# Order of work at three places of a fused macaron block: first block, and both borders between its stages

## What is computed

```python
def reference(x, Wk, bk, Wv, bv, ln_g, ln_b, Wo, bo, W_r, W_k, W_v, mu_r, mu_k):
    def ffn(x):                                   # x is layer-normalized
        x_prev = shift x by one token, zero first
        xr = mu_r * x + (1 - mu_r) * x_prev
        xk = mu_k * x + (1 - mu_k) * x_prev
        return sigmoid(xr @ W_r.T) * (square(relu(xk @ W_k.T)) @ W_v.T)
    def attn(x):                                  # quaternion memory
        keys = unit quaternions of x @ Wk.T + bk
        values = quaternions of x @ Wv.T + bv
        memory = cumsum(quat_mul(values, keys), axis=1)
        retrieved = quat_mul(memory, conj(keys)) / sqrt(position)
        normed = layernorm(retrieved) * ln_g + ln_b
        return x + (normed @ Wo.T + bo)
    x = x + 0.5 * ffn(layernorm(x))
    x = x + attn(layernorm(x))
    return x + 0.5 * ffn(layernorm(x))
```

## Time and profile before

| | us |
|---|---|
| runs of the kernel before: lowest, median, highest of 3 | 669.58, 671.86, 672.56 |
| the profiled execution | 670.52 |
| its span on the core | 668.8 |
| PE busy in the span | 619.1 (93%) |
| DVE, ACT, POOL busy | 561.3, 429.2, 545.2 |

### The profile page before, as it was taken

How to read it: one execution, slowest core, us unless ns; L and a number is a source line. 1 busy time by engine, 2 the same in 40 slices (tenths; PEclk the granted TensorE clock), 3 DMA queues, 4 the chain that set the end, 5 groups by cost and what they waited for, 6 DMA issues and landing times.

```text
span 668.8 us, 12336 instructions
## 1 busy us (share of the span) xinstructions
PE 619.1 (93%) x3412; PEld 524.6 (78%) x3412; DVE 561.3 (84%) x1170; ACT 429.2 (64%) x792; POOL 545.2 (82%) x626
## 2 busy tenths in 40 slices
PE   2899999999978999999999999999767999999997
PEld 2788988988856777777777777777546988998996
DVE  5889999997669999999999999999847877877773
ACT  4576776776456766666676666666354776776762
POOL 3498888887538999999999999999916788889864
PEclk9999999999998999999999999999877999999999
DMA  8730000000000000000000000000000101101111
GB/s 247 236 116 1 0 0 0 0 0 1 1 0 1 0 2 0 0 0 0 0 0 0 0 0 0 0 0 1 0 1 0 65 32 63 63 31 63 63 63 65
DMA packets 19257, 18.66 MB, mean 28 GB/s; under 512 B 1312, under 2 KB 19232, under 8 KB 19232
## 3 DMA queue, kind: packets, MB, share of 16 engines
q1 hardware_dynamic: 19232, 18.36, 8.7%
HBM read 9.97 MB, written 8.39 MB: 27 GB/s over the span
## 4 chain that ended last, share of the span: by engine, by line
PE 79%; DVE 6%; POOL 5%; ACT 5%; issue 4%; DMA 1%; POOLq 0%; DVEq 0%; ACTq 0%
PE bank L1088 25%; PE bank L1119 17%; PE bank L1177 15%; PE bank L1223 7%; PE bank L1102 4%; PE bank L1204 3%; PE bank L1197 3%; ACT m_xnT L822 2%; PE bank L1171 2%; PE bank L1179 2%; DVE diff L404 1%; POOL rhalf L281 1%; POOL bhalf L261 1%; POOL rhalf L282 1%; POOL bhalf L262 1%
## 5 line engine op out<-in xcount | busy, mean ns | idle before, releaser
L1177 PE MATMUL bank<-wkv,m_xnT 128*128 128x256 f32 x512 | 132.7, 389 | 11.4 <-ACT m_xnT L822 11.4
L1119 PE MATMUL bank<-wffn,kact 128*128 128x256 f32 x512 | 118.8, 386 | 6.8 <-DVE kact L420 6.8
L1177 PEld LDWEIGHTS bank<-wkv,m_xnT 128*128 128x128 f32 x512 | 90.5, 192 | 34.9 <-ACT m_xnT L822 18.5
L1119 PEld LDWEIGHTS bank<-wffn,kact 128*128 128x128 f32 x512 | 96.8, 194 | 19.7 <-issue 7.2
L295 POOL TENSOR_TENSOR xk_lo<-xk,xk_hi 128x1024 fp32r<-128x1024 f32 x30 | 71.1, 2369 | 35.1 <-ACT xk_hi L736 35.1
L992 POOL TENSOR_TENSOR xr_lo<-xr,xr_hi 128x1024 fp32r<-128x1024 f32 x32 | 76.3, 2385 | 14.2 <-ACT xr_hi L742 12.6
L999 POOL TENSOR_TENSOR res<-res,gating_buffers 128x1024 f32 (+1 forms) x31 | 74.8, 2413 | 15.5 <-DVE gating_buffers L427 14.2
L585 DVE TENSOR_TENSOR xn<-bank,khat 128x1024 f32<-128x1024 f32 x64 | 77.7, 1216 | 2.1
L585 DVE TENSOR_TENSOR gating_buffers<-bank,khat 128x1024 f32<-128x1024 f32 x64 | 77.5, 1210 | 0.0
L1088 PE MATMUL bank<-wffn_hi,xr_hi 128*128 128x256 f32 x256 | 72.0, 281 | 0.0
L1088 PE MATMUL bank<-wffn_hi,xr_lo 128*128 128x256 f32 x256 | 71.9, 281 | 0.0
(11 more groups left out here) (127 smaller groups left out, 1595.1 us busy)
## 6 DMA issues: line engine op xcount, KB each, us to landing
res<-x SPq DMA_DIRECT2D x16, 512.0 KB, 4.2
out<-res SPq DMA_DIRECT2D x15, 512.0 KB, 2.9
out<-res SPq DMA_DIRECT2D x2, 256.0 KB, 2.2
wffn<-w_k SPq DMA_DIRECT2D x1, 256.0 KB, 3.9
wffn<-w_r SPq DMA_DIRECT2D x1, 256.0 KB, 4.2
wffn<-w_v SPq DMA_DIRECT2D x1, 256.0 KB, 5.5
wo<-w_o SPq DMA_DIRECT2D x1, 256.0 KB, 6.8
wkv<-w_kv SPq DMA_DIRECT2D x1, 256.0 KB, 6.2
```

Of the source, the lines that this page charges most:

```text
L1119: last = nc.tensor.matmul(dst[:, i, :], x[:, f, i * P:(i + 1) * P], wffn[:, w, f, :], start=f == 0, stop=f == FC - 1)
L1177: nc.tensor.matmul(dst[:, i, :], m_xnT[:, f, i * P:(i + 1) * P], wkv[:, f, col:col + D], start=f == 0, stop=False)
```

## The change

What it does:

- First block. SP issues the load of `wo` before the three FFN weights; `columns` gets a semaphore of its own. PE folds the bias ahead of its first transposes. DVE scales the output weights into a new tile `wo_centred` and prepares the bias before it splits the FFN weights; all later uses read `wo_centred`. In stage 0 xk_lo of the first step comes after both xr mixes, as before, but the bias work between the mixes has gone. ACT copies the bias rows before it evicts the second transposes.
- First step of both FFN stages, DVE: the squares come before the mixes of the next group, and `stats_of(1, 1)` after the receptance mixes instead of before the squares.
- First border. POOL takes `first_power` before `key_low` and `receptance_low` of the last group. DVE takes gating of the last group before `key_unit(0, 0)`; the second `x_scales` and the last `memory_stats` between the products of the first step and `key_sum(0, 1)`; the third `x_variance`, ACT's root and the third `x_scales` lie in the second, second and third memory step.
- Second border. DVE makes xk_lo before the xr mixes, takes the inverse deviation before both, and `stats_of(1, 0)` before `store_x(NP - 1, 1)`. PE takes transposes(0, 1) before output(NP - 1, 1).

The diff, cut to its core ("..." marks what is left out):

```diff
...
         wo = sb("wo", [P, FC, D])
+        wo_centred = sb("wo_centred", [P, FC, D])
         wffn = sb("wffn", [P, 3, FC, D])
...
         consts_in = sem("consts_in")
+        cols_in = sem("cols_in")
         wo_in = sem("wo_in")
...
             load_x(0, 0)
-            sp.dma_start(cols[:, :], columns).then_inc(consts_in, 16)
+            sp.dma_start(cols[:, :], columns).then_inc(cols_in, 16)
+            sp.dma_start(wo[:, :, :], w_o.rearrange("(f p) n -> p f n", p=P)).then_inc(wo_in, 16)
             for i, w in enumerate((w_k, w_r, w_v)):
...
             load_x(1, 0)
-            sp.dma_start(wo[:, :, :], w_o.rearrange("(f p) n -> p f n", p=P)).then_inc(wo_in, 16)
             w_kv_rows = w_kv.rearrange("(f p) n -> p f n", p=P)
...
-                dve.wait_ge(consts_in, 16 * 4)
+                dve.wait_ge(consts_in, 16 * 3)
                 nc.vector.tensor_scalar(cols_less_one[:, :], cols[:, 0:2 * FC], -1.0, None, ALU.add)
...
                                         ALU.subtract).then_inc(bias_lines_ready, 1)
+
+            def scale_output_weights():
+                dve.wait_ge(cols_in, 16)
+                dve.wait_ge(wo_in, 16)
                 for f in range(FC):
-                    nc.vector.tensor_scalar(wo[:, f, :], wo[:, f, :], lng[:, f:f + 1], None, ALU.mult).then_inc(wo_scaled, 1)
-
+                    nc.vector.tensor_scalar(wo_centred[:, f, :], wo[:, f, :], lng[:, f:f + 1], None, ALU.mult).then_inc(wo_scaled, 1)
+                dve.wait_ge(consts_pool, 1)
                 nc.vector.tensor_scalar(eps_pos[:, :], pos[:, :], LN_EPS, None, ALU.mult)
...
                 for f in range(FC):
-                    nc.vector.tensor_tensor(wo[:, f, :], wo[:, f, :], v_flat[:, 3 * D:4 * D], ALU.subtract).then_inc(mem_ready, 1)
+                    nc.vector.tensor_tensor(wo_centred[:, f, :], wo_centred[:, f, :], v_flat[:, 3 * D:4 * D], ALU.subtract).then_inc(mem_ready, 1)
...
-                def first_mix(mixed_key, mixed_half, mixed):
+                def first_mix(mixed_key, key_split, mixed):
...
                     mixed_key()
-                    mix_receptance(0, 0, 0)
-                    mixed_half()
-                    mix_receptance(0, 0, 1)
+                    if stage == 0:
+                        mix_receptance(0, 0, 0)
+                        mix_receptance(0, 0, 1)
+                    key_low(dve, nc.vector, e, 0, 0)
+                    key_split()
+                    if stage == 1:
+                        mix_receptance(0, 0, 0)
+                        mix_receptance(0, 0, 1)
                     mixed()
-                    key_low(dve, nc.vector, e, 0, 0)
...
                             difference(nj, nb)
+                            if first:
+                                square(j, b, 0)
+                                square(j, b, 1)
                             mix_key(nj, nb, 0)
                             mix_key(nj, nb, 1)
-                        if first:
-                            stats_of(1, 1)
-                        square(j, b, 0)
-                        square(j, b, 1)
+                        if not first:
+                            square(j, b, 0)
+                            square(j, b, 1)
                         if mixing:
...
                             mix_receptance(nj, nb, 1)
+                        if first:
+                            stats_of(1, 1)
                         if has(b, 4):
...
-                def first_khat():
+                def first_inverse():
                     key_sum(0, 0)
                     key_inverse(0, 0)
+
+                def first_bind(meanwhile):
                     key_unit(0, 0)
-
-                def first_bind():
                     bind(0, 0, 0)
                     bind(0, 0, 1)
+                    meanwhile()
                     key_sum(0, 1)
...
                             start_last()
+                        if has(b, -1) and not has(b, -2):
+                            x_variance(2, NT - CT, NT)
+                        if has(b, -2) and not has(b, -3):
+                            x_scales(2, NT - CT, NT)
                         if has(b, 1):
...
-                return x_variance, x_scales, first_khat, first_bind, steps, store_x, last_moments, last_scales
+                return x_variance, x_scales, first_inverse, first_bind, steps, store_x, last_moments, last_scales
             stats_of, memory_stats, first_mix, ffn_steps, last_gating, _ = ffn(0)
-            x_variance, x_scales, first_khat, first_bind, mem_steps, store_x, last_moments, last_scales = mem()
+            x_variance, x_scales, first_inverse, first_bind, mem_steps, store_x, last_moments, last_scales = mem()
             nc.vector.memset(ones[:, :], 1.0)
             stats_of(0, 0)
+            scale_output_weights()
+            prepare_memory()
             split_weights_high()
...
             stats_of(0, 1)
-            first_mix(prepare_memory, lambda: None, lambda: None)
+            first_mix(lambda: None, lambda: None, lambda: None)
             split_weights_low(1, 2)
...
             x_variance(1, CT, NT - CT)
-            first_khat()
+            first_inverse()
             last_gating()
-            first_bind()
-            x_scales(1, CT, NT - CT)
-            memory_stats(NJ - 1, 1)
-            x_variance(2, NT - CT, NT)
-            x_scales(2, NT - CT, NT)
+
+            def other_layernorms():
+                x_scales(1, CT, NT - CT)
+                memory_stats(NJ - 1, 1)
+
+            first_bind(other_layernorms)
             stats_of, _, first_mix, ffn_steps, _, last_blocks = ffn(1)
...
             first_mix(last_moments, last_scales, lambda: store_x(NP - 1, 0))
+            stats_of(1, 0)
             store_x(NP - 1, 1)
-            stats_of(1, 0)
             ffn_steps()
...
                     keep_moments(NJ - 1, 1)
-                    x_std_of(1, NT - CT, NT)
-                    act.wait_ge(m["x_scales_done"], 3)
+                    act.wait_ge(m["x_scales_done"], 2)
...
                             key_norm(j + 1, b)
+                        if has(b, -1) and not has(b, -2):
+                            x_std_of(1, NT - CT, NT)
+                        if has(b, -3) and not has(b, -4):
+                            act.wait_ge(m["x_scales_done"], 3)
                         if has(b, 3):
...
             receptance_high(0, 0)
-            evict_xT(0, 1, True)
             act.wait_ge(bias_rows_ready, 1)
...
             nc.scalar.copy(bias3[:, D:], v_flat[:, D:3 * D]).then_inc(bias_rows_ready, 1)
+            evict_xT(0, 1, True)
             ffn_steps(first_normalize, lambda: memory_evict_xT(0, 0))
...
                             residual(*at(j, b, -1))
+                        if stage == 0 and has(b, 1) and not has(b, 2):
+                            first_power()
                         if has(b, 1):
...
                             receptance_low(*at(j, b, 1))
-                        if stage == 0 and has(b, 1) and not has(b, 2):
-                            first_power()
...
-                pe.wait_ge(consts_in, 16 * 4)
+                pe.wait_ge(cols_in, 16)
                 pe.wait_ge(wo_in, 16)
...
                 for f in range(FC):
-                    nc.tensor.matmul(v_flat[:, 3 * D:4 * D], mean_of[:, :], wo[:, f, :], start=f == 0, stop=f == FC - 1)
+                    nc.tensor.matmul(v_flat[:, 3 * D:4 * D], mean_of[:, :], wo_centred[:, f, :], start=f == 0, stop=f == FC - 1)
                 pe.wait_ge(bias_lines_ready, 1)
...
                         for f in range(FC):
-                            nc.tensor.matmul(o_bank[:, i, :], normedT[:, f, i * P:(i + 1) * P], wo[:, f, :],
+                            nc.tensor.matmul(o_bank[:, i, :], normedT[:, f, i * P:(i + 1) * P], wo_centred[:, f, :],
                                              start=f == 0, stop=False)
...
             pe.wait_ge(consts_pool, POOL_CONSTS)
+            fold_bias()
             transposes(0, 0)
-            fold_bias()
             bias_rows()
...
                 ret_transposes(NP - 1, 1)
+                transposes(0, 1)
                 output(NP - 1, 1)
-                transposes(0, 1)
                 pe.wait_ge(rprod_done[1], MS)
...
```

## The result

The changed kernel took 664.12 us (median; 663.03 to 664.54 in four runs) against 670.72 for the kernel before on the same chip (669.57 to 672.56, four runs): a ratio of 0.990, 95% interval 0.988 to 0.992, or 7.0 us of 670.7 (6.6 by the medians). The forecast was 660.1 with a range of 655.5 to 667.0 and 0.88 for faster by over 0.5%.

The account below looks back on a forecast made before the run. PE was taken to bound the kernel, with 79% of the chain, leaving time only where it idles or runs at half clock. Terms -1.9 - 4.6 - 5.3 = -11.8 us from 671.86 gave 660.1; range 655.5 to 667.

Parts of the forecast that it names:

- First block: -1.9 predicted: First block: second key pass starts at 33.6 instead of 35.54, a gain of 1.9 us.
- DVE reaches the end of these statistics at new 29.5: First block: DVE ends the moved stats_of(1, 1) at 29.5, where it was before, so xk_lo is ready at 33.6.
- I take nothing: First block: no clock loss charged for PE's idleness of about 2.8 us before the second key pass; other bound 1.5.
- First border: -4.6 predicted: First border: PE's lead into the memory loop grows by 4.6 us, between ends of -5.3 and -4.0.
- leave the path: First border: third x_variance and x_scales leave the path; DVE runs them as 0.16 and 0.5 us in memory steps.
- Second border: -5.3 predicted: Second border: second key pass starts 7.9 us earlier, less 2.6 charged for half clock, giving -5.3; bounds -7.9 and -3.2.
- The PE gap is then 2.3 us for 4.04, like the 2.27 that kept the clock, so the key pass takes 2.8 and not 5.5: -2.7: Second border, first key pass of stage 1: the shorter PE gap keeps full clock, gaining 2.7 us.
- The moved stats_of(1, 1) pays this back: First block: POOL's inverse_std(1, 1) awaits the moved statistics with xk_lo queued behind, making xk_lo ready 1.7 + 2.37 us later.
- (a): Rival: clock falls in every new gap, also before the first block's second key pass; -7.6, 664.3 us; chance 0.25.
- (b): Rival: clock falls in none of the new gaps; -15.1, 656.8 us; chance 0.15.
- (c): Rival: moved statistics and single POOL queue leave 0 in first block, -1.3, -1.7; -3.0, 668.9 us; chance 0.11.
- (d): Rival: slower, POOL's operations meet DVE's reads more often in memory steps, 0.6 us a step; 676 us; chance 0.04.

Follow-up runs that it names:

- the part alone: The kernel before with only the first block's part of the change (early output weights, bias work before the weight split, squares before the mixes in stage 0): 671.39 us, ratio 1.000.
- early split: The changed kernel with DVE's second low split of FFN weights ahead of key_low instead of behind it: 660.23 us, ratio 0.984.
- the first border alone: The kernel before with only the first border's part of the change: 667.18 us, ratio 0.995.
- 28 useless products: The changed kernel with 28 small useless matmuls in PE's idle times before the first key pass of the first block: 664.1 us, ratio 0.990.
- early split with POOL's order: The changed kernel with DVE's second low split ahead of key_low, and POOL's key_low before inverse_std(1, 1) in both FFN stages' first step: 653.85 us, ratio 0.975.
- POOL's order: The changed kernel with POOL's first step of both FFN stages reordered to key_low(0, 1), inverse_std(1, 1), receptance_low(0, 1): 655.49 us, ratio 0.976.
- useless products in stage 1: The changed kernel with 16 useless matmuls of 512 columns in PE's gap before the second key pass of stage 1: 661.46 us, ratio 0.987.
- The run that was to isolate this: The changed kernel with useless matmuls in two PE gaps, before the second memory step's projections and before the last sum_after: 665.65 us, ratio 0.992.
- early split with 28 products: The changed kernel with DVE's second low split ahead of key_low and 28 useless matmuls before the first key pass: 660.5 us, ratio 0.984.
- statistics: The changed kernel with stats_of(1, 1) of both FFN stages right behind the squares, ahead of the xk and xr mixes: 655.58 us, ratio 0.978.
- second border alone: The kernel before with only the second border's part of the change, including the squares before the mixes: 667.72 us, ratio 0.995.

## Why the prediction was right in its sign and too large

**First block: -1.9 predicted, 0 by the median of the part alone, +1.5 in the profiled execution.** The working of each engine's order was right up to 19 us: fold in PE's idle start (6.58), bias work under the wait for the last weight, first key pass at 19.28. Two steps failed. The first is "DVE reaches the end of these statistics at new 29.5": it took DVE's split at its duration from the trace of before, where POOL's xr_lo began 0.10 us after it. The new order let POOL begin 0.15 us ahead, and the split took 2.86. The early split shows this as the cause: the statistics were at POOL at 29.01, the key pass at 33.10 for 33.6 predicted. The second is "I take nothing" for the clock. It fell in the change after 3.06 us of idleness and stayed up with the early split after 2.81; had I not lost the 2.2, that step would have held as well. The bound that I kept for it, 1.5, was near the 1.6 measured.

The rule of the Trainium skill that I weighed ("TensorE: Matmul & The Clock Gate", "What's actually happening": throttled is the default, activity releases it) is borne out by a row. The first twelve products took 24.54 - 19.28 = 5.26 us in the change and 25.70 - 22.18 = 3.52 before: of 2.9 us of earlier start 1.7 went at 1.2 GHz (granted clock 0.50 from 20 to 24 us). By the rule alone I had put the block at -1.1. But this cost is hidden: what sets the second key pass is POOL's queue, not the end of the first.

**First border: -4.6 predicted, -3.6 by the median, -3.3 at the marks.** first_power in POOL's gap, m_xn without a wait, khat 3.6 and 1.3 earlier less what the statistics take: counted from where the border really started, khat was due at 196.4 + 1.5 = 197.9 and came at 197.60. The clock fell in the new gap, which was my lower bound of -4.0, and at 206.36 (before: 208.95) the lead over the start was -4.1, just that. The step that failed is "leave the path": x_var, x_rstd, x_gain and x_shift in the memory steps, for which I had 0.16 and 0.5 us. DVE has no slack in these first steps. Between kinv and khat were 209.07 - 208.09 = 0.98 and 0.98 us before, and 1.36 and 1.77 in the change: 1.2 us together, and the lead shrank by 1.2 between 206 and 225 before it recovered 0.3. About half of this is the collision of the first block once more. In the change x_shift took 0.74 us instead of 0.16 beside an operation of POOL, as in three other kernels (0.73 to 0.74; the first border alone, 28 useless products, early split with POOL's order); where DVE was not held, with the early split, with POOL's order and in two more whose clock fell at the same place, it took 0.16, from kinv to khat were 1.2 us instead of 1.8, and the stretch from the transposes to the output near 470 was 273.8 us long instead of 274.3 to 274.4. So 0.6 us hangs on how DVE and POOL meet there, and only the rest is what the four operations cost by themselves. (In the kernel with useless products in stage 1 x_shift was not held either, and the clock fell one block of four products later; there the stretch was 273.1.) x_gain at 175.00, which took 1.91 beside POOL's xr_lo instead of 0.17, cost nothing, since PE came to the transposes at 178.60 by itself.

**Second border: -5.3 predicted, -3.2 by the median, -4.3 at the marks.** All four parts of the sum are there: xk_lo first, 2.33 us of idleness that in this execution kept the clock, the squares early, and 3.90 us before the second key pass that cost 2.4 of the 2.6 I had charged. What I had not in the sum is the half clock at 479.23, after 2.23 us of idleness at 477.62. In the kernel before the clock had fallen one step earlier, at 473.69, where nobody waited. In the change the two blocks of the output took 3.70 us, where the same two took 2.02 before the gap (471.90 to 473.92), and the transposes behind them, which ACT's xn would have let go at 481.5, came at 482.93: of a lead of 1.73 only 0.50 was left. The run that was to isolate this filled the gap too full, but the other kernels price it. From the output near 470 to the first key pass of stage 1 no edit touches anything, and the stretch is 18.26 us long in the change and 18.26 to 18.27 in the three others whose clock fell here (early split, early split with 28 products, statistics), and 16.99 or 17.00 in the four in which it fell one step earlier, where nobody waits (471.90 to 490.16 against 467.46 to 484.46 in POOL's order). The fall at this place costs 1.26 us.

The step that held by luck is "The PE gap is then 2.3 us for 4.04, like the 2.27 that kept the clock, so the key pass takes 2.8 and not 5.5: -2.7". Of eleven kernels with this order of stage 1, seven kept the clock over the gap of 2.33 us and four lost it (second border alone, 28 useless products, POOL's order, and early split with POOL's order): there 11.0 to 11.1 us pass from the key pass to the value pass instead of 9.59, that is 1.4 to 1.5 more. These are the four with 17.0 us before it. So the clock fell at one of the two places in eight of the nine kernels without useless products at the borders, 27.9 to 28.1 us from the output to the value pass, and only the kernel with useless products in stage 1 got past both, in 26.88, and its products come later than either place. A fall at one or the other was the common case, and the sum had none. Why it falls at one and not at the other no run here shows. The term itself was 0.3 too large as well: by the timeline of before this key pass took 497.67 - 492.39 = 5.28 us and not the chain's 5.49, so a full clock was worth 2.4.

**The cost that I named and did not price against its alternative.** "The moved stats_of(1, 1) pays this back", "bites as in the first block": the mechanism stands in the prediction with its times, POOL waiting for the statistics with xk_lo queued behind, and POOL's other order shows what it costs, 8.6 us. It was right as a step of the sum. It was also the sentence that said that one move of the change takes away more than the whole change gains, and I had not worked that out.

**Rivals.** (a), clock falls in every new gap, 664.3, is the number that came out, but not by its road: the clock fell before the second key pass of the first block and at the first border as it says, and kept up in the 2.33 us gap before 490.16, where it had put 2.1 more and where four other kernels did lose it; the rest came from the collision, the scales in the DVE chain and 479.23. (b) is refuted by these falls, which are also a sign of being wrong that I had named: a granted clock of 0.50 in other places than the second key pass of stage 1 (36 to 38, 200 to 202 and 480 to 482 us). (c), the first block at 0, is right for the first block and wrong for the rest, where -3.6 and -3.2 stand for its -1.3 and -1.7. (d) has nothing: the memory step is 8.99 us (243.53 to 252.52), as long as before.

## What to carry to other kernels

When an order is laid out by hand, it is not enough to give each instruction its old duration: look which instruction of POOL starts within some tenths of a microsecond of each DVE instruction with two operands in SBUF, and of small ones such as x_gain and x_shift, because here 0.15 us decided over 2.2. Before a producer is moved back, ask what stands behind its consumer in that consumer's queue: a small POOL operation that waits holds the large one behind it, and swapping the two was worth more than the whole change.

## What the runs showed of the hardware

DVE and POOL don't slow each other in proportion; one waits for nearly the whole of the other. The split took 0.68 to 0.69 us when it began before POOL's xr_lo (19.87 against 19.97 before; 18.52 against 18.53 with the statistics moved) and 2.85 to 2.87 when POOL had begun first by 0.10 to 0.16 us, in six kernels. In the first case POOL paid: xr_lo took 2.79 and 2.92 instead of 2.37. A small x_gain of 128x8, with one tile as operand, paid in the same way, 1.91 for 0.17. The Trainium skill ("SBUF — State Buffer", "SBUF: two separate sides") has it so, an exclusive lock on the pair of ports that both share, kept for the whole instruction by the one that started first; the trace agrees in the order and in the size.

The clock does not fall at the same gap in every execution. The value pass of the first block, which began after 2.27 us of idleness in the kernel before, took 3.69 us there; with the second border alone changed, which leaves this block as it was, it began after 2.79 and took 5.38. 2.81 us in another kernel kept the clock, 3.06 and more lost it in the change, and at 499.60 of the kernel with the statistics moved it fell after only 1.05 us, with another 0.75 shortly before. The gap of 2.33 us before the first key pass of stage 1 is the plainest case: the same wait for the same tile kept the clock in seven kernels and lost it in four. So a forecast that hangs on one such gap is open by the 0.9 to 2.4 us that the falls cost here.
